# One-core attention and quantised linear block (16 batches): values alone between scores, small products regrouped, tail products added

## The reference, cut to what matters

```python
mod = (silu(c) @ wmod).reshape(16, 6, 1, 128)   # sa, ca, ga, sb, cb, gb: one row of 128 per batch
ga, gb = (sign(g) * max(abs(g), 0.25) for g in (ga, gb))
h = layernorm(x) * (1 + ca) + sa
q, k, v = split(h @ W_qkv + b_qkv)              # 16 heads of 8
attn = softmax(q @ k.T, axis=-1) / sqrt(128)    # per head, 256 x 256
x = x + ga * ((attn @ v) @ W_out + b_out)
h = layernorm(x) * (1 + cb) + sb
x = x + gb * (mx_quantise(h) @ mx_quantise(W).T + bias)   # blocks of 32 share a scale, FP6 grid
```

## Time and profile before

| what | value |
|---|---|
| median of 3 runs | 273.32 us (272.11 to 274.05) |
| the profiled execution | 273.2 us |
| its span, first to last instruction | 271.4 us |
| mean granted TensorE clock | 0.99 of full speed |
| PE busy | 252.9 us, 93% |
| DVE busy | 233.0 us, 86% |
| ACT busy | 205.9 us, 76% |
| POOL busy | 185.3 us, 68% |
| HBM read and written | 22.88 and 9.99 MB |

### The profile page before, as it was taken

The page is one execution under the profiler, slowest core; times in us unless marked ns, Lnnn a source line. Parts: engine busy times, 40 slices in busy tenths (PEclk is TensorE's granted clock), DMA queues, the critical chain, the costliest instruction groups (busy, mean ns, idle before and its releaser), DMA issues.

```text
span 271.4 us, 7574 instructions
## 1 busy us (share of the span) xinstructions
PE 252.9 (93%) x2568; PEld 165.2 (61%) x2568; DVE 233.0 (86%) x597; ACT 205.9 (76%) x414; POOL 185.3 (68%) x384
## 2 busy tenths in 40 slices
PE   2679999999999999999999999999999999999952
PEld 2356666666676666666666666666667666565631
DVE  6579997999899999999999999999998889852264
ACT  5255787978797879797979888887978777777620
POOL 5814071869777878787878888797978655637550
PEclk9999999999999999999999999999999999999996
DMA  5465577364726555364637362627263630100000
GB/s 140 119 184 156 148 231 194 108 172 141 191 86 174 163 138 161 101 208 129 185 96 193 117 182 93 196 98 195 93 180 109 179 116 24 45 24 22 0 31 31
DMA packets 21654, 34.94 MB, mean 129 GB/s; under 512 B 3408, under 2 KB 17504, under 8 KB 19696
## 3 DMA queue, kind: packets, MB, share of 16 engines
q1 hardware_dynamic: 18688, 31.71, 40.1%
q10 hardware_dynamic: 2928, 2.75, 3.3%
HBM read 22.88 MB, written 9.99 MB: 121 GB/s over the span
## 4 chain that ended last, share of the span: by engine, by line
PE 78%; DVE 9%; issue 3%; DMA 3%; SPq 2%; ACTq 2%; POOL 1%; ACT 1%; POOLq 0%; DVEq 0%
PE ps_p L1026 26%; PE ps_o L1056 21%; PE ps_pre L1078 5%; PE ps_p L1041 5%; PE ps_post L1109 3%; DVE neg_max L837 3%; PE ps_o L1095 3%; PE ps_post L1123 3%; PE ps_pre L1085 2%; PE ps_p L1156 2%; PE ps_pre L1072 2%; PE ps_post L1117 2%; PE ps_pre L1065 2%; DMA q_rows<-maxT 1%; ACTq L393 1%
## 5 line engine op out<-in xcount | busy, mean ns | idle before, releaser
L837 DVE TENSOR_REDUCE neg_max<-ps_p 128x2 f32<-128x512 f32 x256 | 164.1, 681 | 10.5 <-PE ps_p L1026 9.0
L653 ACT ACTIVATE probs<-ps_p 128x512 f32<-128x512 f32 x256 | 139.3, 596 | 20.6 <-PE ps_p L1041 16.4
L1026 PE MATMUL ps_p<-k_rows,q_rows 62*128 62x256 f32 x512 | 97.9, 307 | 0.7 <-DVE neg_max L837 0.4
L1041 PE MATMUL ps_p<-q_rows,k_rows 64*128 64x256 f32 x512 | 98.1, 308 | 0.4 <-DMA q_rows<-maxT 0.4
L1026 PEld LDWEIGHTS ps_p<-k_rows,q_rows 62*128 62x128 f32 x512 | 69.2, 185 | 29.8 <-DVE neg_max L837 12.9
L1041 PEld LDWEIGHTS ps_p<-q_rows,k_rows 64*128 64x128 f32 x512 | 69.7, 185 | 4.7 <-ACT probs L653 2.3
L1056 PE MATMUL ps_o<-probs,v_aug 128*32 128x256 f32 x1024 | 68.5, 385 | 0.3 <-ACT probs L653 0.3
L1056 PEld LDWEIGHTS ps_o<-probs,v_aug 128*32 128x32 f32 x1024 | 26.7, 109 | 20.0 <-ACT probs L653 0.8
L499 POOL CAST max_parts<-neg_max 128x16 fp32r<-128x16 f32 x32 | 6.3, 197 | 40.1 <-DVE neg_max L837 40.1
L525 POOL TENSOR_TENSOR qk_parts<-qk_full_sb,qk_parts 128x256 fp32r<-128x256 f32 x28 | 20.4, 730 | 2.3
L1078 PE MATMUL ps_pre<-hT,wqk_sb 128*128 128x256 f32 x56 | 17.9, 402 | 1.8 <-ACT hT L623 1.0
(11 more groups left out here) (142 smaller groups left out, 360.1 us busy)
## 6 DMA issues: line engine op xcount, KB each, us to landing
q_rows<-q_dram SPq DMA_DIRECT2D x30, 256.0 KB
k_rows<-k_dram SPq DMA_DIRECT2D x60, 128.0 KB
modb<-mod_rows_dram SPq DMA_DIRECT2D x16, 256.0 KB, 3.7
q_dram<-qk_parts SPq DMA_DIRECT2D x28, 128.0 KB, 2.4
k_dram<-qk_parts SPq DMA_DIRECT2D x28, 128.0 KB, 2.4
out_dram<-out_sb SPq DMA_DIRECT2D x16, 128.0 KB, 1.8
x_all<-in_L_attn_x_dram ACTq DMA_DIRECT2D x6, 256.0 KB, 4.4
q_rows<-maxT SPq DMA_DIRECT2D x64, 8.0 KB
```

Source lines behind the costliest of these rows:

```text
L653: act.activation(probs[:, v % 2, u % 4, :], ps_p2[:, (16 * b + u) % P2_BANKS, :], ACT.Exp).then_inc(exp_done, 1)
L837: dve.tensor_reduce(neg_max[:, half, :, r, j], ps_p1[:, (16 * b + s) % P1_BANKS, :].rearrange("p (q k) -> p q k", q=QT), AX_X, ALU.max, ne ...
L1026: ins = pe.matmul(ps_p1[:, (16 * b + s) % P1_BANKS, t * T:(t + 1) * T], q_rows[64 * r:64 * r + ROWS1, slot, i, t * P:(t + 1) * P], k_rows[ ...
L1041: ins = pe.matmul(ps_p2[:, (16 * b + u) % P2_BANKS, t * T:(t + 1) * T], k_rows[64 * r:64 * r + ROWS2, slot, i, t * P:(t + 1) * P], q_rows[ ...
```

## The change

- PE: the four `values` groups of a step stand alone. Behind the other pairs of scores there are: at position 2 the heads' transposes and `linear(b - 3)`; at 4 q, k and norm; at 8 the maxima of half 0, v and out; at 14 hd, x of batch c+1 and the maxima of half 1. `linear` and its copy `hdT` are thus a step later than before, and `finish(b - 3)` goes from position 0 to 4 of its step.
- The bank of `ps_pre` is used in two halves: `ps_pre_b` takes x, k and v. ACT's reads wait for the last product into the bank: hT for the maxima of half 1, q for k, the maxima of half 0 for v.
- ACT: hT at position 2, q at 5, norm's copy at 6, k at 7, the maxima of half 0 at 9 (before at 7), v at 10, hdT at 0.
- SP: the output's store goes ahead of half 0 of the maxima.
- POOL: `quantise` goes ahead of `ffn_weights`. `x1b` has two buffers.
- `nm` goes: the means are subtracted where the negated means were added.
- Head: hT of batch 1 is copied ahead of k's first two DMAs; batch 3's statistics on DVE go ahead of the modulation rows; k's product of batch 2 goes from behind the first to behind the second pair of first-pass scores.
- Tail: 2, 1 and 8 unread products of 128 columns (`unread_last`).

The diff, cut to its core:

```diff
@@ -173,7 +170,8 @@
-        ps_pre = ps("ps_pre", [P, 512])[:, 0:T]
+        ps_pre_bank = ps("ps_pre", [P, 512])
+        ps_pre, ps_pre_b = ps_pre_bank[:, 0:T], ps_pre_bank[:, T:2 * T]
...
@@ -327,8 +325,8 @@
-                ins = eng.tensor_scalar(xh2[:, n, :], x1[:, n, :], nm2[:, n:n + 1], rstd2[:, n:n + 1],
-                                        ALU.add, ALU.mult)
+                ins = eng.tensor_scalar(xh2[:, n, :], x1[:, n, :], mv2[:, n, 0:1], rstd2[:, n:n + 1],
+                                        ALU.subtract, ALU.mult)
...
@@ -457,10 +455,10 @@
                     load_modb(b + 1)
+                if has(b - 3):
+                    store(b - 3)
                 if has(b + 1):
                     place_max(b + 1, 0)
-                if has(b - 3):
-                    store(b - 3)
                 if in_steps(c):
...
@@ -543,8 +540,8 @@
-                wait(pool, (bffn_b_ready, b + 1), (out_ready, b))
-                pool.tensor_tensor(x1b[:, :, :], x1[:, :, :], bffn_b[:, :].unsqueeze(1).to_broadcast([P, QT, E]),
+                wait(pool, (bffn_b_ready, b + 1), (out_ready, b - 1))
+                pool.tensor_tensor(x1b[:, b % 2, :, :], x1[:, :, :], bffn_b[:, :].unsqueeze(1).to_broadcast([P, QT, E]),
...
@@ -576,8 +573,8 @@
                 if has(b - 2) and b - 2 != LAST:
+                    quantise(pool, b - 2)
                     ffn_weights(b - 2)
-                    quantise(pool, b - 2)
                     residual2(b - 2)
...
@@ -617,10 +614,10 @@
-            def save_hT(c):
-
-                wait(act, (xT_full, c + 1), (v_full, c - 2))
-                act.activation(hT[:, c % 3, :], ps_pre[:, :], ACT.Identity, scale=scaleT[:, c:c + 1],
+            def save_hT(c, src=ps_pre, *before):
+
+                wait(act, (xT_full, c + 1), (v_full, c - 2), *before)
+                act.activation(hT[:, c % 3, :], src, ACT.Identity, scale=scaleT[:, c:c + 1],
                                bias=shiftT[:, c:c + 1]).then_inc(hT_saved, 1)
...
@@ -628,10 +625,10 @@
-            def save_qk(c, kind, full, saved):
+            def save_qk(c, kind, full, saved, src=ps_pre):
                 wait(act, (full, c + 1), (low_ready, 2 * (c - FIRST - 1) + kind + 1))
-                act.activation(qk_full_sb[:, kind, :], ps_pre[:, :], ACT.Identity, bias=bqkv_col[:, kind:kind + 1]
+                act.activation(qk_full_sb[:, kind, :], src, ACT.Identity, bias=bqkv_col[:, kind:kind + 1]
                                ).then_inc(saved, 1)
...
@@ -640,8 +637,8 @@
-            def save_maxT(b, half):
-                wait(act, (maxT_full, 2 * b + half + 1), (max_placed[half], 32 * b))
+            def save_maxT(b, half, *before):
+                wait(act, (maxT_full, 2 * b + half + 1), (max_placed[half], 32 * b), *before)
...
@@ -664,8 +661,8 @@
             first_qk(0, 1, k_full)
+            save_hT(1)
             place_first(act, 1, 0, 0)
-            save_hT(1)
             place_first(act, 1, 0, 1)
...
@@ -691,6 +688,8 @@
                         exponentials(b, s)
+                    if s == 0 and has(b - 3) and b - 3 < LAST - 2:
+                        save(b - 3, hdT_full, f_full, hdT[:, :], ps_post[:, :], hdT_saved)
                     if s == 1 and b - 1 == LAST:
...
@@ -698,34 +697,36 @@
                         save(b - 1, pv_done, o_full, oT[:, :], ps_o[:, :], oT_saved, 4)
-                    if s == 1 and pre:
-                        save_hT(c)
-                    if s == 3 and pre:
-                        save_qk(c, 0, q_full, q_saved)
+                    if s == 2 and pre:
+                        save_hT(c, ps_pre_b, (maxT_full, 2 * b + 2))
+                    if s == 5 and pre:
+                        save_qk(c, 0, k_full, q_saved)
                     if s == 5 and b - 1 == LAST:
...
                         save(b - 2, hdT_full, f_full, hdT[:, :], ffn_psum(b - 2), hdT_saved)
-                    elif s == (5 if in_steps(c) else 7) and has(b - 1) and b - 1 != LAST:
+                    elif s == (6 if in_steps(c) else 7) and has(b - 1) and b - 1 != LAST:
                         save(b - 1, onT_full, y_full, onT[:, :], ps_post[:, :], onT_saved)
-                    if s == 5 and pre:
-                        save_qk(c, 1, k_full, k_saved)
-                    if s == 7 and has(b + 1):
-                        save_maxT(b + 1, 0)
+                    if s == 7 and pre:
+                        save_qk(c, 1, k_full, k_saved, ps_pre_b)
+                    if s == 7 and b == -1:
+                        save_maxT(0, 0)
+                    if s == 9 and has(b + 1) and b >= 0:
+                        save_maxT(b + 1, 0, (v_full, b + 2))
                     if s == 11 and b == -1:
...
                         load_x(act, b + 6)
-                    if s == 9 and has(b + 1) and b >= 0:
-                        save_v(b + 1)
+                    if s == 10 and has(b + 1) and b >= 0:
+                        save_v(b + 1, ps_pre_b)
                     if s == 13 and b - 2 == LAST:
...
                                       (f_full, LAST))
-                    elif s == 13 and has(b - 2) and b - 2 != LAST - 1:
+                    elif s == 13 and b - 2 == LAST - 2:
                         save(b - 2, hdT_full, f_full, hdT[:, :], ps_post[:, :], hdT_saved)
...
@@ -746,10 +747,9 @@
-            def finish_stats(mv, nm, ve, aggregated, value):
+            def finish_stats(mv, ve, aggregated, value):
...
-                dve.tensor_tensor(nm[:, :], mv[:, :, 0], minus_one[:, :], ALU.mult)
...
@@ -813,6 +813,9 @@
+            stats1(FIRST + 1)
+            aggregate1(FIRST + 1)
+
             dve.wait_ge(rows_copied, 1)
...
@@ -825,8 +828,6 @@
-            stats1(FIRST + 1)
-            aggregate1(FIRST + 1)
...
@@ -963,7 +964,7 @@
                             finish_last(t)
-                    elif s == 0 and has(b - 3) and b - 3 != LAST - 1:
+                    elif s == (0 if b - 3 == LAST - 2 else 4) and has(b - 3) and b - 3 < LAST - 1:
                         finish(b - 3)
...
@@ -1059,10 +1060,10 @@
-            def transpose_x(c, *before):
+            def transpose_x(c, dst, *before):
                 wait(pe, (xhat_ready, c + 1), *before)
                 for n in range(QT):
-                    ins = pe.transpose(ps_pre[:, n * P:(n + 1) * P], xhat[:, c % 2, n, :], ident[:, :])
+                    ins = pe.transpose(dst[:, n * P:(n + 1) * P], xhat[:, c % 2, n, :], ident[:, :])
                 ins.then_inc(xT_full, 1)
...
@@ -1160,16 +1161,21 @@
-            transpose_x(0)
+            def unread_last(dst, n):
+
+                for _ in range(n):
+                    pe.matmul(dst[:, 0:P], ident[:, :], ident[:, :], start=True, stop=True)
+
+            transpose_x(0, ps_pre)
             pe.wait_ge(wqk_ready, 1)
...
             project_qk(0, 1, k_full, ps_p2[:, 1, 0:T])
-            transpose_x(1, (hT_saved, 1))
+            transpose_x(1, ps_pre, (hT_saved, 1))
             pe.wait_ge(wmod_rows_loaded, 16)
...
             project_qk(1, 1, k_full, ps_p2[:, 1, 0:T], (first_low, 2))
-            transpose_x(FIRST, (hT_saved, FIRST))
+            transpose_x(FIRST, ps_pre, (hT_saved, FIRST))
             project_v(0, ps_p1[:, 1, 0:T])
...
@@ -1200,23 +1206,26 @@
                             scores2(b, u, 1)
-                    if b == -2 and s == 12:
+                    if b == -2 and s == 14:
                         project_qk(FIRST, 1, k_full, ps_pre[:, :], (q_saved, 1))
...
                         values(b - 1, 3)
-                    if s == 0 and pre:
-                        transpose_x(c, (maxT_saved, 2 * (b + 1)), (v_saved, 1))
+                        if b - 1 == LAST:
+                            pe.wait_ge(max_done, 16 * NB)
+                            unread_last(ps_p1[:, 0], 2)
                     if s == 2 and b - 1 == LAST:
...
                             transpose_o_last(t)
+                        unread_last(ps_p1[:, 0], 1)
                     elif s == 2 and has(b - 1):
                         transpose_o(b - 1)
-                    if s == 2 and pre:
-                        project_qk(c, 0, q_full, ps_pre[:, :])
+                    if s == 2 and has(b - 3) and b - 3 < LAST - 2:
+                        linear(b - 3)
                     if s == 4 and pre:
-                        project_qk(c, 1, k_full, ps_pre[:, :], (q_saved, c - FIRST + 1))
+                        project_qk(c, 0, q_full, ps_pre[:, :], (maxT_saved, 2 * (b + 1)))
+                        project_qk(c, 1, k_full, ps_pre_b)
                     if s in (2, 4) and b in (LAST - 2, LAST) or s == 4 and b == LAST - 1:
...
@@ -1227,16 +1236,17 @@
                         values(b, 0)
-                    if s == 6 and has(b + 1):
+                    if s == (6 if b == -1 else 8) and has(b + 1):
                         transpose_max(b + 1, 0, (k_saved, c - FIRST + 1) if in_steps(c) else (maxT_saved, 2 * (b + 1)))
+                    if s == 8 and has(b + 1) and b >= 0:
```

(10 more changed lines are left out.)

30 lines of the change are left out of this document (13 added, 17 removed).

## The result

The changed kernel takes 285.3 us (median of 4 runs, 282.9 to 288.1), the kernel before beside it 273.7. The ratio is 1.042, with an interval from 1.029 to 1.054: slower, as forecast, but by more than the 2.3% forecast, and 0.3 us outside the range. The profiled execution took 286.55 us for a span of 284.7.

What follows compares the result with a forecast made beforehand. PE was taken as the bound at 14.2 us a step, the maxima's loop almost as long; +8.4 - 0.8 - 0.6 - 0.1 - 0.75 = +6.2 on 273.2 gave 279.4 us, 2.3% slower, range 267.5 to 285.

Steps and rivals of the forecast that it cites:

- Part 5: Tail and nm: two small VectorE operations per batch go, -0.1 us; unread products hold the clock in the tail, -0.75 or 0.
- Part 4: Steps 13 to 15: only regrouping gains, -0.6 us; two x1b buffers and finish at position 4: 0, between -0.3 and +0.5.
- the loop of the maxima: S8, transposed maxima, ScalarE's copy, SyncE's half 0, stores and layouts, half 1, next S8: forecast 14.9 us a step.
- PE bounds, and the maxima's loop stands close behind it: Before the change, PE's work sets the 14.2 us steps; the loop through the row maxima's copy is almost as long.
- Part 1: Regrouping on PE: fewer costly first products outside the values, 4.04 to 3.57 us; PE's step falls 0.47, to 13.75.
- Rival D: Regrouping gains nothing: PE's step stays 14.2 us under a 14.9 loop, 279.4 us again; chance 0.58 together with the forecast.
- Part 2: Half 0 of the maxima issued 1.6 us later after S8, loop 14.9 us against 14.2, over 13 steps: +8.4 us.
- X: Time on SyncE's queue from issuing half 0 of the maxima to landing of half 1: taken as 13.1 us (12.1 to 13.6).
- the +8.4 of the sum: The maxima loop's term: 13 x (14.9 - 14.2) = +9.1 us, less 0.7 for the earliest steps.
- no new wait there: GpSimd's weights behind the quantising: q's and k's parts come 0.9 us later, q's store 1.2 later, so no added wait.
- Head -0.8: Head: k's product of batch 2 behind the second scores pair -0.7 us, batch 3's statistics -0.1 at most; range 0 to -1.5.
- Tail -0.75: Eight unread products keep PE's clock up: 0.5 us off the last linear, 0.25 off transposes, or 0 if the clock falls.

Runs made afterwards that it cites:

- run 1: The changed kernel with nm kept: VectorE's product by minus one and GpSimd's add form put back; 281.4 us, ratio 1.025 to the kernel before.
- run 11: The changed kernel with GpSimd's weights for the linear ahead of the quantising again, as before; 284.7 us, ratio 1.040 to the kernel before.
- run 14: The kernel before with the feed-forward's move (hd 14, linear 2, finish 4, two x1b) and quantise ahead of ffn_weights; ratio 1.019.
- run 5: The kernel before with the change's head and tail edits alone; ratio 0.994 (0.975 to 1.014).
- run 13: The changed kernel with nm kept, the feed-forward where it was and GpSimd's weights ahead of the quantising; ratio 1.035 to the kernel before.
- run 4: run 1 with half 0 of the maxima early, transposed at position 6 and copied at 7; 278.6 us, ratio 1.018 to the kernel before.
- run 2: The kernel before with nm alone removed, the means subtracted instead; 276.0 us, ratio 1.003.
- run 3: The kernel before with subtract for add in xh and xhat, VectorE's product kept but by plus one; 282.2 us, ratio 1.027.
- run 16: The kernel before with the subtract in xh alone; 278.7 us, ratio 1.014.
- run 17: The kernel before with the subtract in xhat alone; 275.3 us, ratio 1.003.

## Why the prediction was right and wrong

Two steps of the prediction failed, both terms set at next to nothing: nm in Part 5 ("-0.1", measured +1.6% of the time in the changed kernel) and the feed-forward's move in Part 4 ("0", measured 1.9% alone). With nm kept (run 1) the change costs 2.5%, beside the 2.3% forecast; without it 4.2%, if with intervals that overlap a little. So the nm term carries the time past the forecast, and it also changes what sets the step: GpSimd's round, not the loop of the maxima.

- **PE bounds, and the maxima's loop stands close behind it: right, and incomplete.** A third loop stood as close: VectorE's residual, GpSimd's layer norm, VectorE's block maxima, with 0.46 us of slack. Rows 1 show VectorE at 13.72 of 14.20 us, and I took that for free time.
- **Part 1, PE's step 14.2 to 13.75: too good while batches are laid out.** In run 1, from 127.76 to 142.50, 14.74 us less the 0.59 of S8's wait are 14.15. The groups outside scores and values fell from 4.61 to 4.39 us, the norm's wait included, half of the forecast 0.47; but scores behind a group no longer run on free, and took 5.76 for 5.61. Rival D, that the gain isn't there, was the better description of these steps. Behind them it is there: from the S8 of step 12 to that of step 14 run 1 takes 28.14 us, the kernel before 28.96.
- **Part 2, loop 14.9: right where it can be seen, and not what sets the change.** Half 0 is issued 2.06 us after S8 in the changed kernel (132.88 less 130.82; forecast 2.1), X, where the copy shows as a wait, is 12.3 to 13.4 in run 1 (13.1), and the loop makes 15.0 us a step there. In the changed kernel GpSimd's round takes 15.1 by itself, and from step 2 on the maxima land in time or nearly. That 0.7 us a step were forecast and 0.8 measured in these ten is the luck of two loops of nearly one length; with step 1 it was 13.9 against the +8.4 of the sum.
- **"no new wait there"** for GpSimd's swap: wrong. GpSimd stands 14.9 us in all for rs (9.3 before), 0.96 in each step of the chain that sets the pace. As a trade it is even: with the later linear the old order waits 15.4 us for wf_b (run 11).
- **Part 4, the finish at position 4: "0": failed.** VectorE's free time at position 4 doesn't exist when the engine is held, in order, by the block maxima. The feed-forward's move alone costs 1.9% with its swap (0.9 to 2.8), 2.5% without; the norm's transposes wait 0.31 us a step for the finish in run 14. In the changed kernel this loop stands behind GpSimd's. The last three steps, forecast -0.6, took 0.2 more.
- **Part 5, nm: "-0.1": failed, the sign was wrong.** Two operations of VectorE did go, but the cost of the new form of xh and xhat was not bounded; the trace of before had no row for it, and I named no range. It measures +0.35 us each. With all else changed it costs about 1.6% (1.042 against run 1's 1.025), in the kernel before 0.3%.
- **Head -0.8: right in the kernel before** (-0.73), -0.4 in the changed kernel's profile. **Tail -0.75: between nothing and -0.7.** Where the clock held to the end (runs 1, 5 and 13) it gave 0.6 to 0.7; in the change 0.4, with a last linear of 0.93 us; in the six traces with one of 1.12 or more 0.2 or less. I chose the better of two ends.
- **The rest of the miss**: step 1 took 5.7 us more in the profiled execution, of it 3.2 a late copy and some 2.5 the half clock after it. The forecast had nothing for a single long wait. X is 14.6 us there (38.98 to 53.62). Run 11, the changed kernel but for GpSimd's order, waits 1.4 us there, runs 1 and 4 1.3 and 0.4; why this execution waits longest isn't settled.

The parts don't add: alone they cost 0.3% (nm), 1.9 (feed-forward with its swap) and 3.5 (q, k, v, x and the maxima; run 13, with head and tail in it), together 4.2. Each lengthens another loop, and the longest counts: GpSimd's round (15.1) in the change, with nm kept the maxima's (15.0) and then one of 14.7.

## What to carry to other kernels

List every loop that closes in one step, with its slack, before moving an instruction: read for each producer when it ends and when its reader starts (0.46 us here), not an engine's busy share. An operation moved behind a waiting one inherits its wait where the engine works in program order, as VectorE does in these traces, and passes it on through the buffers it frees. And bound the cost of any changed opcode, even of add for subtract, or measure it by itself.

## What the runs showed of the hardware that was not expected

- GpSimd's `tensor_scalar` of 128x128 float32 takes 0.45 us as add and multiply and 0.80 as subtract and multiply, whether the scalar lies in mv or in nm (runs 2 and 3; 16 and 17 too). VectorE's own uses of the two forms take the same (0.35).
- A VectorE product of 128x2 takes 0.16 to 0.73 us according to what GpSimd runs beside it; with one such product in each layer norm, 276.0 us became 282.2 (runs 2 and 3).
- Of the twelve traces with unread products in the tail the last linear took 0.71 us in three, 0.80 to 0.93 in three and 1.12 to 1.23 in six; in the seven without them it took 1.22 or 1.23 each time. PE's stand ahead of it was 2.5 to 2.7 us with them, 4.3 to 4.5 without.
